# Cross attention of a decoder layer: two chunks pass each TensorE stage together, and the output projection moves in front of the second pair's scores

## Chip, cores and metric

One core of a Trainium2 chip runs the whole kernel as one program. The metric is the device time of one execution in microseconds (us), lower is better; the times shown are the median of three runs.

## The reference, cut to what matters

A decoder layer for 8 sequences of 256 tokens and width 128: a state-space block, then this cross attention, then six layers of window attention, with a layer norm after each part. Only the cross attention is touched by the change:

```python
lat = layernorm(latents, ln_l_w, ln_l_b)          # latents: x, (8, 256, 128)
ctx = layernorm(context, ln_c_w, ln_c_b)          # context: (8, 256, 128)
q = (lat @ Wq).reshape(b, n, 16, 64).transpose(0, 2, 1, 3)
k, v = jnp.split(ctx @ Wkv, 2, axis=-1)           # heads as for q
attn = jnp.clip(jnp.einsum('bhnd,bhsd->bhns', q, k) * 64 ** -0.5, -11.0, 11.0)
out = jnp.einsum('bhns,bhsd->bhnd', jax.nn.softmax(attn, axis=-1), v)
out = out.transpose(0, 2, 1, 3).reshape(b, n, 1024) @ Wo + bo
x = _layernorm(x + out, axis=-1)
```

## The kernel before

The kernel is written engine by engine: each engine has its own instruction list in an order set by hand, and semaphores alone order the engines against each other. All data is float32. TensorE (PE) writes only to PSUM; ScalarE (ACT), VectorE (DVE) and GpSimd (POOL) do the rest; SyncE (SP) issues the DMAs.

The cross attention works through 64 **chunks** g = 8b + c: batch b of 8, and chunk c of 8, which is a pair of heads (2 x 64 channels = 128 partitions). For a chunk:

- `project(g)` on PE makes q and k of the two heads (L966, L967), in one of the two "misc" PSUM banks `psM`. `copy_qk(g)` on ACT copies them to `qk[g % 2]` (L852).
- `scores(g)` on PE: keys x queries, 64 rows of the array for each head, into two of the four banks `psS` (L982). `exponentials(g)` on ACT writes `E` (L845), one of two slots; `clip(g)` on DVE limits it in place (L899), since clipping after the exponential is the same as before it.
- `sum_of_tiles(g)` on POOL adds the two tiles of keys into `Es` (L794), from which a matmul with ones makes the denominator.
- `times_v(g)` on PE: the values times E (L997), 64 columns of the array for each head, and the denominator (L1001), into one of two banks `psO`.
- `normalise(g)` on DVE: reciprocal of the denominator (L903), and the product into `OT[b % 2, c]` (L904).

For a batch: `statistics`, `deviation`, `hats` (layer norm of latents and context, on DVE and ACT), `transpose_rows` on PE (L958) and `scale_transposed` on ACT into `latT` and `ctxT`; `project_v(b, n)`, four parts, on PE (L973) with `evacuate_v` on ACT (L836); and at its end `out_projection(b, t)`, two tiles t of 128 tokens, 8 matmuls each over the 8 chunks of `OT` (L1012), `residual`, `moments2`, `deviation2`, `finish` (L909 to L918).

All that goes through a `psM` bank (transposes `cat`, `qk`, `v`, `wo`) is a *fill*. The list `fills` gives the order of them, and fill k takes bank k % 2, so each fill waits until the one two places before it was evacuated.

PE's loop over g runs one chunk ahead with projections and one behind with the values: project(g+1), scores(g), times_v(g-1). The batch work is set between: the output projection's first tile of batch b-1 after times_v at c = 1, its second before the scores at c = 2, transposes at c = 3, one value projection at each of c = 4 to 7. The first tile waits for the last normalised chunk of its batch:

```python
if t == 0:
    pe.wait_ge(O_free, (b + 1) * NC)
    ps, full = bank(b, "wo")
```

Names of tiles in the trace: `x_psM`, `x_psS`, `x_psO` are the banks, `x_latT`, `x_ctxT`, `x_qk`, `x_E`, `x_Es`, `x_V`, `x_rden`, `x_OT`, `x_res`, `x_hat` the buffers, `x_wq`, `x_wk`, `x_wv`, `x_wo` the weights. One float32 matmul of the program appears as two weight loads (PEld) and two matmul passes (PE).

Of the kernel before, what the change touches and what calls it, by code (L numbers as in the profile page):

```python
# [17 lines left out]
ALU = mybir.AluOpType  # L18
ACT = mybir.ActivationFunctionType
AX = mybir.AxisListType  # L20

P = 128
B, L, D = 8, 256, 128
TILES = B * L // P
TPB = L // P
# [3 lines left out]
H, DH = 16, 64  # L29
# [651 lines left out]
def cross_attention_block(nc, xall, ident, eps_col, inputs, window):  # L681
# [8 lines left out]
    NC = INNER // P  # L690
    R = 2 * TPB
    LOADS = 16 * 7
    CHUNKS = B * NC
    LO, HI = float(np.exp(-11.0)), float(np.exp(11.0))

    with ExitStack() as ctx:
        def sb(name, shape, dt=F32):
            return ctx.enter_context(nc.sbuf_tensor(name, shape, dt))
# [5 lines left out]
        wq, wk, wv, wo = inputs.wq, inputs.wk, inputs.wv, inputs.wo  # L704
# [8 lines left out]
        ctxT = sb("x_ctxT", [P, 2, L])  # L713
        V1 = sb("x_V1", [P, 2, TPB, H, DH])
        qk = sb("x_qk", [P, 2, 2, L])
        E = sb("x_E", [P, 2, 2, TPB, L])
        Es = sb("x_Es", [P, 2, 2, L])
        rden = sb("x_rden", [P, 2, L])
        OT = sb("x_OT", [P, 2, NC, L])
# [27 lines left out]

        block = ctx.enter_context(nc.Block())

        fills = [(0, "cat"), (0, "qk0")]  # L750
        for g in range(CHUNKS + 1):
            b, c = divmod(g, NC)
            if g + 1 < CHUNKS:
                fills.append(((g + 1) // NC, f"qk{(g + 1) % NC}"))
            if g == 0:
                fills += [(0, f"v{n}") for n in range(4)]
            if c == 1 and b >= 1:
                fills.append((b - 1, "wo"))
            if c == 3 and b + 1 < B:
                fills.append((b + 1, "cat"))  # L760
            if c >= 4 and b + 1 < B:
                fills.append((b + 1, f"v{c - 4}"))
        fills.append((B - 1, "wo"))
        place = {f: (k % 2, k // 2) for k, f in enumerate(fills)}

# [17 lines left out]
        @block.gpsimd  # L783
        def _(pool):
            pool.memset(ones[:, :], 1.0).then_inc(Es_ready, 1)
            pool.memset(window.xsA[0:1, 0, 64:D], 0.0)
            pool.wait_ge(loaded, LOADS)

            def sum_of_tiles(g):
                pool.wait_ge(E_ready, 2 * g + 2)  # L790
                if g >= 2:

                    pool.wait_ge(O_full, g - 1)
                pool.tensor_tensor(Es[:, g % 2, :, :], E[:, g % 2, :, 0, :], E[:, g % 2, :, 1, :], ALU.add).then_inc(Es_ready, 1)  # L794

            def add_bias(b):
                if b >= 1:

                    pool.wait_ge(finished, b)
                pool.tensor_tensor(res[:, :, :], xall[:, b * TPB:(b + 1) * TPB, :], bo[:, :].unsqueeze(1).broadcast_to([P, TPB, D]), ALU.add).then_inc(res_ready, 1)  # L800

            for g in range(CHUNKS):
                b, c = divmod(g, NC)
                sum_of_tiles(g)
                if c == NC - 1:
                    add_bias(b)
            pool.wait_ge(window.loaded, 32)
            pool.tensor_scalar(window.base_tab[:, :, 0, :, :], window.base_tab[:, :, 0, :, :], 8.0, None, ALU.mult)

        @block.scalar  # L810
        def _(act):
            act.preload_act_table_set(LN_EXP)
            act.wait_ge(loaded, LOADS)
            chain = Chain(act, act_chain, 0, 0)

            def deviation(b):
                act.wait_ge(mom_ready, b + 1)
                chain(act.activation(lnv[:, :], mom[:, :, 1], ACT.Ln, bias=eps_col))
                act.activation(rstd[:, :], lnv[:, :], ACT.Exp, scale=-0.5).then_inc(rstd_ready, 1)

            def deviation2(b):
                act.wait_ge(mom2_ready, b + 1)
                chain(act.activation(lnv2[:, :], mom2[:, :, 1], ACT.Ln, bias=eps_col))
                act.activation(rstd2[:, :], lnv2[:, :], ACT.Exp, scale=-0.5).then_inc(rstd2_ready, 1)

            def scale_transposed(b):
                ps, free = wait_fill(act, b, "cat")
                act.activation(ctxT[:, b % 2, :], ps[:, L:2 * L], ACT.Identity, bias=cols[:, 3:4], scale=cols[:, 2:3])
                act.activation(latT[:, b % 2, :], ps[:, 0:L], ACT.Identity, bias=cols[:, 1:2], scale=cols[:, 0:1]).then_inc(free, 1)

            def evacuate_v(b, n):
                ps, free = wait_fill(act, b, f"v{n}")
                if b >= 2 and n == 0:

                    act.wait_ge(O_full, (b - 1) * NC)
                act.activation(V1[:, b % 2, n // 2, (n % 2) * 8:(n % 2) * 8 + 8, :],  # L836
                               ps[:, :].rearrange("p (h d) -> p h d", d=DH), ACT.Copy).then_inc(free, 1)

            def exponentials(g):
                for j in range(2):  # L840
                    act.wait_ge(S_full, 2 * g + j + 1)
                    if j == 0 and g >= 2:

                        act.wait_ge(O_full, g - 1)
                    act.activation(E[:, g % 2, j, :, :], psS[(2 * g + j) % 4][:, :, :], ACT.Exp, scale=DH ** -0.5).then_inc(E_exp, 1)  # L845

            def copy_qk(g):
                ps, free = wait_fill(act, g // NC, f"qk{g % NC}")
                if g >= 2:

                    act.wait_ge(S_full, 2 * g - 2)
                act.activation(qk[:, g % 2, :, :].rearrange("p a t -> p (a t)"), ps[:, :], ACT.Copy).then_inc(free, 1)  # L852

            deviation(0)
            scale_transposed(0)
            copy_qk(0)
            for g in range(CHUNKS + 1):
                b, c = divmod(g, NC)
                if g + 1 < CHUNKS:
                    copy_qk(g + 1)  # L860
                if g < CHUNKS:
                    exponentials(g)
                if g == 0:
                    for n in range(4):
                        evacuate_v(0, n)
                if c == 1 and b + 1 < B:
                    deviation(b + 1)
                if c == 3 and b >= 1:
                    deviation2(b - 1)
                if c == 3 and b + 1 < B:  # L870
                    scale_transposed(b + 1)
                if c >= 4 and b + 1 < B:
                    evacuate_v(b + 1, c - 4)
            deviation2(B - 1)

        @block.vector
        def _(dve):
# [18 lines left out]
            def clip(g):  # L896
                for j in range(2):
                    dve.wait_ge(E_exp, 2 * g + j + 1)
                    dve.tensor_scalar(E[:, g % 2, j, :, :], E[:, g % 2, j, :, :], LO, HI, ALU.max, ALU.min).then_inc(E_ready, 1)  # L899

            def normalise(g):
                dve.wait_ge(O_full, g + 1)
# [17 lines left out]

            statistics(0)
            hats(0)
            for g in range(CHUNKS + 1):
                b, c = divmod(g, NC)
                if c == 2 and b >= 1:
                    residual(b - 1)
                if g < CHUNKS:
                    clip(g)
                if g >= 1:
                    normalise(g - 1)  # L930
                if c == 0 and b + 1 < B:
                    statistics(b + 1)
                if c == 2 and b + 1 < B:
                    hats(b + 1)
                if c == 2 and b >= 1:
                    moments2(b - 1)
                if c == 4 and b >= 1:
                    finish(b - 1)
            residual(B - 1)
            moments2(B - 1)  # L940
# [3 lines left out]
        def _(pe):  # L944
# [41 lines left out]
            def times_v(g):  # L986
# [7 lines left out]
                    pe.wait_ge(O_free, g - 1)  # L994
                for kt in range(TPB):
                    for j in range(2):
                        pe.matmul(psO[g % 2][j * DH:(j + 1) * DH, 0, :], V1[:, b % 2, kt, 2 * c + j, :], E[:, g % 2, j, kt, :],  # L997
                                  start=(kt == 0), stop=(kt == TPB - 1), skip_group_check=True)
                pe.wait_ge(Es_ready, g + 2)
                for j in range(2):  # L1000
# [14 lines left out]

            transpose_rows(0)
            project(0)
            for g in range(CHUNKS + 1):
                b, c = divmod(g, NC)
                if g + 1 < CHUNKS:  # L1020
                    project(g + 1)
                if c == 2 and b >= 1:
                    out_projection(b - 1, 1)
                if g < CHUNKS:
                    scores(g)
                if g == 0:
                    for n in range(4):
                        project_v(0, n)
                if g >= 1:
                    times_v(g - 1)  # L1030
                if c == 1 and b >= 1:
                    out_projection(b - 1, 0)
                if c == 3 and b + 1 < B:
                    transpose_rows(b + 1)
                if c >= 4 and b + 1 < B:
                    project_v(b + 1, c - 4)
            out_projection(B - 1, 0)
            out_projection(B - 1, 1)

# [973 lines left out]
```

## Time and profile before

| | |
|---|---|
| median of 3 runs | 2365.95 us (2365.91 to 2366.62) |
| profiled execution | 2364.26 us |
| its span, first to last instruction | 2362.5 us |
| PE / DVE / ACT / POOL busy | 93% / 79% / 72% / 70% |
| mean granted TensorE clock | 0.983 |
| cross attention | from about 326 us to 622 us of the span |

Shares are over the whole span, of which the cross attention is about an eighth. A matmul's end in the profile is modelled, so the start times of weight loads tell PE's pace better than durations do. PEld is the weight load, which can run ahead of the matmul before it. A bracket at the end of a line is the time the engine sat idle before it and what ended that.

### The profile page before, as it was taken

Reading aid. Unit: us, or ns where it says so; the run is one execution under the profiler, and the core shown is the slowest. Engines: PE = TensorE matmul, PEld = TensorE weight load, DVE = VectorE, ACT = ScalarE, POOL = GpSimd, SP = SyncE. Lnnn points to the kernel's source line nnn. Section 1 sums busy time; section 2 is a strip of 40 time slices with the busy share of each in tenths; the row PEclk is TensorE's granted clock in tenths of the full one; section 3 lists DMA queues with packets and bytes.
Section 4 is the critical chain, followed back from the end, with each engine's and each line's share of the span. In section 5 each row is a group of like instructions: output and inputs, shape, how many; then the busy total and the mean of one; then the engine's idle time right before and its main releaser. Section 6 shows DMA issues by size and latency. Waiting matters only on the chain. (4 is left out here: it accounts for less than half of the span.)

```text
span 2362.5 us, 70312 instructions
## 1 busy us (share of the span) xinstructions
PE 2204.0 (93%) x26385; PEld 1467.1 (62%) x26385; DVE 1860.9 (79%) x2680; ACT 1707.2 (72%) x3299; POOL 1648.2 (70%) x1553
## 2 busy tenths in 40 slices
PE   5889779999799999999999999999999999999996
PEld 3555446666456666666666666666666666666664
DVE  4899957777678878888888888888888887888884
ACT  5889734544377787787787787787778778778774
POOL 4777833333478778778788787787787787787872
PEclk8999989999999999999999999999999999999997
DMA  2311210000022222222222222222222222322221
GB/s 74 113 58 66 72 52 2 1 1 1 20 63 67 55 78 67 59 74 67 65 69 67 69 64 67 73 60 67 77 55 68 79 54 68 79 53 72 75 53 52
DMA packets 103196, 140.36 MB, mean 59 GB/s; under 512 B 63072, under 2 KB 64096, under 8 KB 102752
## 3 DMA queue, kind: packets, MB, share of 16 engines
q1 hardware_dynamic: 103136, 139.57, 21.8%
q8 instruction: 36, 0.59, 0.1%
q14 instruction: 24, 0.20, 0.0%
HBM read 56.39 MB, written 1.31 MB: 24 GB/s over the span
## 5 line engine op out<-in xcount | busy, mean ns | idle before, releaser
L1802 PE MATMUL f_psA<-f_W,f_xT 128*128 (+1 forms) x1152 | 600.7, 631 | 21.1 <-DVE f_m L1607 13.4
L1607 DVE TENSOR_TENSOR f_m<-f_psA,f_tab 128x1024 f32<-128x1024 f32 x384 | 461.1, 1222 | 119.5 <-ACT f_sq L1468 106.3
L1357 POOL TENSOR_TENSOR f_Pr<-f_Pr,f_rden 128x384 f32<-128x384 f32 x384 | 311.0, 831 | 226.2 <-DVE f_rden L1586 226.2
L1385 POOL TENSOR_TENSOR f_qkr<-f_qkr,f_rn 128x1024 f32<-128x1024 f32 x192 | 361.2, 1902 | 0.2 <-POOL f_rn L1393 0.2
L1802 PEld LDWEIGHTS f_psA<-f_W,f_xT 128*128 128x128 f32 x1152 | 188.3, 189 | 162.9 <-issue 112.5
L1468 ACT ACTIVATE f_sq<-f_psA 128x512 f32<-128x512 f32 x384 | 228.0, 594 | 78.6 <-PE f_psA L1802 75.7
L1773 PEld LDWEIGHTS f_psO<-f_PT,f_V 96*64 96x64 f32 x6144 | 203.7, 138 | 96.5 <-issue 88.4
L1375 POOL TENSOR_TENSOR f_qkr<-f_m 128x512 f32<-128x512 f32 x192 | 244.1, 1271 | 8.2 <-DVE f_m L1607 8.2
L1376 POOL TENSOR_TENSOR f_qkr<-f_m 128x512 f32<-128x512 f32 x192 | 244.5, 1273 | 0.0
L1773 PE MATMUL f_psO<-f_PT,f_V 96*64 96x64 f32 x6144 | 232.1, 228 | 1.8 <-ACT f_PT L1443 1.8
L794 POOL TENSOR_TENSOR x_Es<-x_E 128x512 f32<-128x512 f32 x64 | 81.0, 1266 | 205.8 <-DVE x_E L899 205.8
L1622 DVE TENSOR_REDUCE f_ssq<-f_sq 128x32 f32<-128x2048 f32 x96 | 218.5, 2276 | 0.0
L1460 ACT ACTIVATE f_Pr<-f_Pr 128x768 f32<-128x768 f32 x192 | 162.2, 845 | 55.4 <-DVE f_Pr L1580 53.8
L1869 PE MATMUL f_psO<-f_W,f_oT 128*128 (+1 forms) x1536 | 196.9, 281 | 0.8 <-ACT f_oT L1456 0.8
L284 POOL TENSOR_TENSOR m_Hs<-m_Hs,m_Cb 128x1024 f32<-128x1024 f32 x64 | 151.3, 2370 | 64.4 <-DVE m_Hs L472 64.4
L1452 ACT ACTIVATE f_Vt<-f_psA 128x512 f32<-128x512 f32 x192 | 114.5, 597 | 112.0 <-PE f_psA L1802 107.1
L1580 DVE TENSOR_TENSOR f_Pr<-f_psS,f_mx 128x768 f32<-128x768 f32 x192 | 183.8, 957 | 10.7
L1573 DVE TENSOR_REDUCE f_mx<-f_psS 128x8 f32<-128x768 f32 x192 | 178.3, 929 | 14.3 <-PE f_psS L1741 8.6
L1869 PEld LDWEIGHTS f_psO<-f_W,f_oT 128*128 128x128 f32 x1536 | 178.7, 191 | 7.3 <-issue 0.9
L1584 DVE TENSOR_REDUCE f_den<-f_Pr 128x8 f32<-128x768 f32 x192 | 179.9, 937 | 3.9 <-ACT f_Pr L1460 3.9
L1417 POOL TENSOR_SCALAR f_hatC<-f_xsC,f_momC,f_rstdC 128x128 f32<-128x128 f32 x96 | 77.1, 803 | 136.9 <-ACT f_rstdC L1544 136.9
L1806 PE MATMUL f_psD<-f_xnT,f_W 128*128 128x256 f32 (+1 forms) x576 | 163.6, 395 | 1.4 <-issue 0.8
(167 smaller groups left out, 4894.6 us busy)
## 6 DMA issues: line engine op xcount, KB each, us to landing
f_V<-f_Vt SPq DMA_DIRECT2D x96, 384.0 KB, 4.2
f_V<-f_Vt SPq DMA_DIRECT2D x96, 256.0 KB, 3.6
f_W<-in_f_W SPq DMA_DIRECT2D x48, 344.0 KB, 3.4
m_Cb<-m_BC_rows SPq DMA_DIRECT2D x64, 256.0 KB, 3.1
f_W<-in_f_W SPq DMA_DIRECT2D x48, 296.5 KB, 4.0
f_V<-f_Vt SPq DMA_DIRECT2D x48, 128.0 KB, 5.3
f_xsA<-xall SPq DMA_DIRECT2D x97, 32.0 KB
f_xsA<-xall SPq DMA_DIRECT2D x97, 31.8 KB
```

The lines of the kernel that those rows point to most:

```text
L1357: pool.tensor_tensor(pv, pv, rv.unsqueeze(3).broadcast_to([P, 2, 2, KEYS]), ALU.mult).then_inc(Pr_ready[g][j], 1)
L1375: pool.tensor_tensor(qv[:, :, 0, :], mv[:, 0, :, 0, :], mv[:, 1, :, 1, :], ALU.add)
L1376: pool.tensor_tensor(qv[:, :, 1, :], mv[:, 0, :, 1, :], mv[:, 1, :, 0, :], ALU.add).then_inc(rot_done[j], 1)
L1385: pool.tensor_tensor(qv, qv, rv.unsqueeze(3).broadcast_to([P, 2, GH, DH]), ALU.mult).then_inc(qkr_ready[g], 1)
L1468: act.activation(sq[:, n * 512:(n + 1) * 512], psA[n % 2][:, :], ACT.Square).then_inc(squared[n], 1)
L1580: dve.tensor_tensor(Pr[:, g, :, :].rearrange("p (a c) k -> p a c k", a=2), S4, mb, ALU.subtract).then_inc(S_free[g], 1)
L1584: dve.tensor_reduce(den[:, g, :], Pr[:, g, :, :], axis=AX.X, op=ALU.add).then_inc(den_done[g], 1)
L1607: dve.tensor_tensor(m12[:, j, :, half].rearrange("p m (h d) -> p m h d", d=DH), psA[n % 2][:, :].rearrange("p (h d) -> p h d", d=DH).unsqu ...
L1622: dve.tensor_reduce(ssq[:, :], sq[:, :].rearrange("p (h d) -> p h d", d=DH), axis=AX.X, op=ALU.add).then_inc(ssq_ready, 1)
L1773: ins = pe.matmul(psO[(h % 2) * DH:(h % 2) * DH + DH, h // 2, half * HQ:(half + 1) * HQ], V96[:, tile, half, hh_ * DH:(hh_ + 1) * DH], PT[ ...
L1802: pe.matmul(psA[n % 2][:, :], xT[:, t, :], weights(i, W_QKV + n * 512, 512), start=True, stop=True).then_inc(A_full[n_fill], 1)
L1869: ins = pe.matmul(psO[:, 0, :], oT[:, t, c, :], weights(i - 1, W_O + c * D, D), start=(c == 0), stop=(c == CH - 1))
```

## The change

All four engine lists take two chunks at a time (g, g+1; the loop step is 2). PE: scores(g), scores(g+1), times_v(g-2), times_v(g-1), project(g+2), project(g+3). `E` gets four slots, and the exponentials of chunk g wait for the values of chunk g-4 only. DVE's order in a pair is clip(g), normalise(g-2), clip(g+1), normalise(g-1). Both tiles of the output projection of batch b-1 stand in front of the scores at c = 2, directly behind the projections of the pair with c = 0. The transposes stand at c = 2, two value projections each at c = 4 and c = 6; hats and scale_transposed move to c = 2, deviation2 to c = 4, finish to c = 6. The list of fills follows.

```diff
+    ES = 4
-        E = sb("x_E", [P, 2, 2, TPB, L])
+        E = sb("x_E", [P, ES, 2, TPB, L])
...
-        fills = [(0, "cat"), (0, "qk0")]
-        for g in range(CHUNKS + 1):
+        fills = [(0, "cat"), (0, "qk0"), (0, "qk1")]
+        for g in range(0, CHUNKS + 1, 2):
             b, c = divmod(g, NC)
-            if g + 1 < CHUNKS:
-                fills.append(((g + 1) // NC, f"qk{(g + 1) % NC}"))
+            if c == 2 and b >= 1:
+                fills.append((b - 1, "wo"))
             if g == 0:
                 fills += [(0, f"v{n}") for n in range(4)]
-            if c == 1 and b >= 1:
-                fills.append((b - 1, "wo"))
-            if c == 3 and b + 1 < B:
+            if g + 2 < CHUNKS:
+                fills += [((g + 2) // NC, f"qk{(g + 2) % NC}"), ((g + 3) // NC, f"qk{(g + 3) % NC}")]
+            if c == 2 and b + 1 < B:
                 fills.append((b + 1, "cat"))
             if c >= 4 and b + 1 < B:
-                fills.append((b + 1, f"v{c - 4}"))
+                fills += [(b + 1, f"v{c - 4}"), (b + 1, f"v{c - 3}")]
...
-                    if j == 0 and g >= 2:
-                        act.wait_ge(O_full, g - 1)
+                    if j == 0 and g >= ES:
+                        act.wait_ge(O_full, g - ES + 1)
...
             deviation(0)
             scale_transposed(0)
             copy_qk(0)
-            for g in range(CHUNKS + 1):
+            copy_qk(1)
+            for g in range(0, CHUNKS + 1, 2):
                 b, c = divmod(g, NC)
-                if g + 1 < CHUNKS:
-                    copy_qk(g + 1)
                 if g < CHUNKS:
                     exponentials(g)
+                    exponentials(g + 1)
                 if g == 0:
                     for n in range(4):
                         evacuate_v(0, n)
-                if c == 1 and b + 1 < B:
+                if g + 2 < CHUNKS:
+                    copy_qk(g + 2)
+                    copy_qk(g + 3)
+                if c == 0 and b + 1 < B:
                     deviation(b + 1)
-                if c == 3 and b >= 1:
+                if c == 2 and b + 1 < B:
+                    scale_transposed(b + 1)
+                if c == 4 and b >= 1:
                     deviation2(b - 1)
-                if c == 3 and b + 1 < B:
-                    scale_transposed(b + 1)
                 if c >= 4 and b + 1 < B:
                     evacuate_v(b + 1, c - 4)
+                    evacuate_v(b + 1, c - 3)
...
             statistics(0)
             hats(0)
-            for g in range(CHUNKS + 1):
+            for g in range(0, CHUNKS + 1, 2):
                 b, c = divmod(g, NC)
+                if c == 2 and b + 1 < B:
+                    hats(b + 1)
                 if c == 2 and b >= 1:
                     residual(b - 1)
                 if g < CHUNKS:
                     clip(g)
-                if g >= 1:
+                if g >= 2:
+                    normalise(g - 2)
+                if g < CHUNKS:
+                    clip(g + 1)
+                if g >= 2:
                     normalise(g - 1)
                 if c == 0 and b + 1 < B:
                     statistics(b + 1)
-                if c == 2 and b + 1 < B:
-                    hats(b + 1)
                 if c == 2 and b >= 1:
                     moments2(b - 1)
-                if c == 4 and b >= 1:
+                if c == 6 and b >= 1:
                     finish(b - 1)
...
             transpose_rows(0)
             project(0)
-            for g in range(CHUNKS + 1):
+            project(1)
+            for g in range(0, CHUNKS + 1, 2):
                 b, c = divmod(g, NC)
-                if g + 1 < CHUNKS:
-                    project(g + 1)
                 if c == 2 and b >= 1:
+                    out_projection(b - 1, 0)
                     out_projection(b - 1, 1)
                 if g < CHUNKS:
                     scores(g)
+                    scores(g + 1)
                 if g == 0:
                     for n in range(4):
                         project_v(0, n)
-                if g >= 1:
+                if g >= 2:
+                    times_v(g - 2)
                     times_v(g - 1)
-                if c == 1 and b >= 1:
-                    out_projection(b - 1, 0)
-                if c == 3 and b + 1 < B:
+                if g + 2 < CHUNKS:
+                    project(g + 2)
+                    project(g + 3)
+                if c == 2 and b + 1 < B:
                     transpose_rows(b + 1)
                 if c >= 4 and b + 1 < B:
                     project_v(b + 1, c - 4)
+                    project_v(b + 1, c - 3)
```

In the other places where `E` is used, `g % 2` becomes `g % ES`.

## Rows read from the trace of the kernel before

**Rows 1.** The page: span, and busy us with share and instructions of each engine.

```profile
span 2362.5 us, 70312 instructions
PE 2204.0 (93%) x26385; PEld 1467.1 (62%) x26385; DVE 1860.9 (79%) x2680; ACT 1707.2 (72%) x3299; POOL 1648.2 (70%) x1553
```

**Rows 2.** Windows: length, busy PE, PEld, DVE, ACT, POOL; granted clock, DMA share, GB/s.

```profile
333.00:612.00 279.00, 278.53 (x1825) 174.45 (x1823) 207.34 (x386) 137.30 (x263) 84.57 (x71) 1.00 0.01 2
...
612.00:620.00 8.00, 5.41 (x44) 4.30 (x44) 4.17 (x4) 0.00 (x0) 2.81 (x3) 1.00 0.00 0
...
635.00:645.00 10.00, 7.45 (x34) 2.54 (x35) 5.52 (x5) 5.19 (x8) 6.52 (x5) 0.66 0.29 72
```

**Rows 3.** Waits from 333 to 612 us: us in total, times, longest.

```profile
PEld x_psO L997 <- issue: 20.9, 63, 0.3
PEld x_psM L966 <- issue: 20.7, 75, 0.4
PEld x_psS L982 <- issue: 18.3, 55, 0.4
```

**Rows 4.** Timeline of two chunks of batch 7: start us, us, engine, line, instructions.

```profile
583.91 0.30 PEld L966 LDWEIGHTS x_psM<-x_latT,x_wq 128*128 128x128 f32 x2 [0.38 <-issue]
...
584.24 0.41 PEld L967 LDWEIGHTS x_psM<-x_ctxT,x_wk 128*128 128x128 f32 x2
...
584.98 0.73 PEld L982 LDWEIGHTS x_psS<-x_qk 64*128 64x128 f32 x8 [0.33 <-issue]
...
585.08 0.60 ACT L852 ACTIVATE x_qk<-x_psM 128x512 f32<-128x512 f32 x1 [1.43 <-PE x_psM L967]
586.04 0.63 PEld L997 LDWEIGHTS x_psO<-x_E,x_V 128*64 128x64 f32 x8 [0.33 <-issue]
...
586.14 1.09 ACT L845 ACTIVATE x_E<-x_psS 128x512 f32<-128x512 f32 x2 [0.46 <-PE x_psS L982]
...
586.77 0.92 DVE L899 TENSOR_SCALAR x_E<-x_E 128x512 f32<-128x512 f32 x2 [0.52 <-ACT x_E L845]
...
587.49 1.86 PEld L1012 LDWEIGHTS x_psM<-x_wo,x_OT 128*128 128x128 f32 x16 [0.38 <-issue]
...
587.61 1.75 DVE L903 RECIPROCAL x_rden<-x_psO 128x256 f32<-128x256 f32 x1
...
589.27 0.30 PEld L966 LDWEIGHTS x_psM<-x_latT,x_wq 128*128 128x128 f32 x2
...
589.39 0.42 DVE L904 TENSOR_TENSOR x_OT<-x_psO,x_rden 128x256 f32<-128x256 f32 x1
...
592.23 0.42 DVE L909 TENSOR_TENSOR x_res<-x_res,x_psM 128x256 f32<-128x256 f32 x1 [2.41 <-PE x_psM L1012]
```

**Rows 5.** Timeline of batch 0's value projections and of batch 1's first chunks.

```profile
333.94 0.30 PEld L973 LDWEIGHTS x_psM<-x_wv,x_ctxT 128*128 128x128 f32 x2 [0.66 <-ACT x_V L836]
...
370.39 0.47 DVE L47 BATCH_NORM_STATS2 x_stats<-xall 128x6 f32<-128x128 f32 x2
...
371.40 0.38 DVE L51 BATCH_NORM_AGGREGATE x_mom<-x_stats 128x2 f32<-128x6 f32 x4
...
376.45 0.42 DVE L909 TENSOR_TENSOR x_res<-x_res,x_psM 128x256 f32<-128x256 f32 x1 [1.90 <-PE x_psM L1012]
```

**Rows 6.** Timeline of the last chunks, to the last output projection.

```profile
604.02 0.59 DVE L918 TENSOR_SCALAR xall<-x_res,x_mom,x_rstd 128x128 f32<-128x128 f32 x2
...
606.40 0.73 PEld L982 LDWEIGHTS x_psS<-x_qk 64*128 64x128 f32 x8 [0.33 <-issue]
...
611.16 0.75 DVE L899 TENSOR_SCALAR x_E<-x_E 128x512 f32<-128x512 f32 x2
611.83 1.75 DVE L903 RECIPROCAL x_rden<-x_psO 128x256 f32<-128x256 f32 x1
...
615.81 0.42 DVE L904 TENSOR_TENSOR x_OT<-x_psO,x_rden 128x256 f32<-128x256 f32 x1
616.29 3.65 PEld L1012 LDWEIGHTS x_psM<-x_wo,x_OT 128*128 128x128 f32 x32 [2.77 <-DVE x_OT L904]
```

More of the change, by code:

```diff
@@ L793, in sum_of_tiles @@
                     pool.wait_ge(O_full, g - 1)
-                pool.tensor_tensor(Es[:, g % 2, :, :], E[:, g % 2, :, 0, :], E[:, g % 2, :, 1, :], ALU.add).then_inc(Es_ready, 1)
+                pool.tensor_tensor(Es[:, g % 2, :, :], E[:, g % ES, :, 0, :], E[:, g % ES, :, 1, :], ALU.add).then_inc(Es_ready, 1)
             def add_bias(b):
@@ L841, in exponentials @@
                     act.wait_ge(S_full, 2 * g + j + 1)
-                    if j == 0 and g >= 2:
-                        act.wait_ge(O_full, g - 1)
-                    act.activation(E[:, g % 2, j, :, :], psS[(2 * g + j) % 4][:, :, :], ACT.Exp, scale=DH ** -0.5).then_inc(E_exp, 1)
+                    if j == 0 and g >= ES:
+                        act.wait_ge(O_full, g - ES + 1)
+                    act.activation(E[:, g % ES, j, :, :], psS[(2 * g + j) % 4][:, :, :], ACT.Exp, scale=DH ** -0.5).then_inc(E_exp, 1)
             def copy_qk(g):
@@ L898, in clip @@
                     dve.wait_ge(E_exp, 2 * g + j + 1)
-                    dve.tensor_scalar(E[:, g % 2, j, :, :], E[:, g % 2, j, :, :], LO, HI, ALU.max, ALU.min).then_inc(E_ready, 1)
+                    dve.tensor_scalar(E[:, g % ES, j, :, :], E[:, g % ES, j, :, :], LO, HI, ALU.max, ALU.min).then_inc(E_ready, 1)
             def normalise(g):
@@ L996, in times_v @@
                     for j in range(2):
-                        pe.matmul(psO[g % 2][j * DH:(j + 1) * DH, 0, :], V1[:, b % 2, kt, 2 * c + j, :], E[:, g % 2, j, kt, :],
+                        pe.matmul(psO[g % 2][j * DH:(j + 1) * DH, 0, :], V1[:, b % 2, kt, 2 * c + j, :], E[:, g % ES, j, kt, :],
                                   start=(kt == 0), stop=(kt == TPB - 1), skip_group_check=True)
```

## The prediction

> **What bounds the kernel now.** I read the page's busy times and granted clock first: TensorE (PE) is busy 93% of the span at a mean clock of 0.983 [rows 1]. Then the stretches of the cross attention, because the diff touches nothing else: 279 us in which PE is busy without a gap at the full clock, VectorE (DVE) 74%, ScalarE (ACT) 49%, GpSimd (POOL) 30% [rows 2]. So its price is PE's time, plus whatever pause a new order makes. Six batches, from one residual addition to the one six batches later, take 592.23 - 376.45 = 215.78 us, 35.96 each [rows 4, 5].
>
> A busy PE need not be streaming. The waits of that stretch show a pause of the weight loads, with no releaser ("issue"), in front of nearly every stage: 63 before the values, 75 before the projections, 55 before the scores [rows 3]. The timeline gives its price. First loads of one chunk: projection 583.91, scores 584.98, values 586.04, output projection 587.49, so stages of 1.06, 1.06 and 1.45 us, 3.57 in all [rows 4]. Inside a stage, 256-column passes follow each other at 0.215 us (two loads in 0.41 us, less 0.19 for one [rows 4]). Projection and scores have 4 such steps (0.86), the values with the denominator 6 (1.29). Each entry to a stage thus costs 0.20, 0.20 and 0.155 us more than staying in it: 0.555 for the three.
>
> The pause belongs to the stage, not to the chunk: the projection that follows the output projection, both 128*128, loads at 589.27 with no pause, though it is another chunk's work behind its own semaphore, while each border between 128*128, 64*128 and 128*64 has one [rows 4].
>
> The Trainium skill (TensorEngine Tiling (Array Packing), Key Properties) has a rule for this: a change of the tiling mode drains TensorE, and the trace agrees. For the size, the skill (TensorE: Matmul & The Clock Gate, Single matmul latency) puts what a lone matmul can't overlap at 166 ns at the full clock; as an estimate by that page the 93 entries below would save 15.4 us and the sum would be +5.8. The rows have the entry itself, 0.185 on average, and decide.
>
> **What the change removes.** Two chunks share each entry. Before, scores are entered 64 times, values 63; after, 32 and 31. Up to the last pair of scores, 31 entries of each kind go: 31 x 0.555 = **-17.2 us**. A pair with nothing added then takes 1.92 + 2.74 + 1.92 = 6.59 us. Number and size of matmuls, activations and vector operations are unchanged; there are no new DMAs, and SP's queue has only its wait for the first finished batch, far ahead of need.
>
> **What it adds: the wait of the output projection.** Call T the first scores load of a pair with c = 0. PE works scores(g), scores(g+1) to T+1.92, values of chunks 6 and 7 of the last batch to T+4.66, two projections to T+6.28, and now stands before the output projection, which needs the normalised chunk 7. Before, its first tile came behind a whole further chunk (PE's load of it at 587.49 shows no wait for `x_OT` [rows 4]). DVE's order is clip(g), normalise(g-2), clip(g+1), normalise(g-1):
> - The reciprocal starts 1.57 us after the values' first load (586.04 to 587.61): T+1.92+1.57 = T+3.49. clip(g), at +1.79 (584.98 to 586.77) for 0.92 us, is out of the way.
> - Reciprocal to multiplication 1.78, multiplication 0.42: T+5.69 [rows 4].
> - clip(g+1) to the next reciprocal 0.67 (611.16 to 611.83) [rows 6]: T+6.36; again 1.78 + 0.42: T+8.56; to the waiting load 0.06 (616.23 to 616.29) [rows 6]: T+8.62.
>
> The load is 8.62 - 6.28 = 2.34 us late. On-time loads stand 0.215 ahead of their matmul, the first two loads of a fresh stage only 0.11 apart (0.30 less 0.19 [rows 4]), so 0.10 is cover: a pause of 2.23 us, 7 times (the eighth is the tail): **+15.6 us**. Bounds: if the second reciprocal waited only for its matmuls (T+1.92+1.29+1.57 = 4.78, plus 2.26), the load would be due at T+7.04, pause 0.66, 4.6 us in all; if the clip pair took its 0.92 instead of 0.67, 2.5 each, 17.4. I take the chain, since program order fixes it. Nothing fills the pause: scores(g+2) is queued behind on PE, and ACT and DVE wait for those scores.
>
> **Bank waits.** The misc banks are two, and after a pair of projections the third fill (transposes at c = 2, value projection at c = 4 and 6) needs the copy of the first. That copy starts 1.17 us after the projection's first load and takes 0.60 [rows 4], and a load follows its release by 0.05 (as at 616.29, 0.06 [rows 6]): T+4.66+1.82 = 6.48 against 6.28 due. 0.2 late, 0.10 of it covered: 0.1 x 3 x 7 = **+2.1 us**, bounds 0 and 4.2. Where scores follow directly, the stage entry covers the copy (6.48 against 6.59), and the second chunk's copy ends with nothing to spare: 0.86 later, 7.34, against a load due at 6.59 + 0.76 = 7.35.
>
> **Start.** In g = 0 four value projections stand behind both pairs of exponentials (2 x 1.09 us on ACT), and they already wait for evacuations (0.66 us of load pause) [rows 5]. Evacuation starts a microsecond later, of which the second scores stage takes most: **+0.2 us**, bounds 0 and 0.6.
>
> **Tail.** From the last pair of scores, at W: normalise(60) ends W+5.69, clip(63), normalise(61) W+8.56, then finish(6), now moved here, 0.59 for its two operations [rows 6], reciprocal W+9.17, normalise(62) W+11.37, normalise(63) W+13.57, output projection W+13.63. values(62) can go at W+5.75 and values(63) at W+8.62, so they end before DVE wants them. Before, from scores(62) at 606.40 the projection came at 616.29, 9.89 later [rows 6]. At W one projection more is done (0.86) and one value stage fewer (1.29): W stands 0.43 earlier. 13.63 - 9.89 - 0.43 = **+3.3 us**; bounds 2.5 (clip and finish hidden) and 4. The tail after that is unchanged.
>
> **Edits at nothing.** Statistics (370.39 to 371.78, 1.39 us [rows 5]) run in the output projection's pause and stage: they end T+9.9, the deviation with its 0.52 us T+10.4, and hats T+11.6, before clip(g+2) is due at about T+14. Moving scale, hats, moments and finish leaves DVE its slack: its pair of clips and normalisations ends at +8.56, that is +1.97 of the next pair, where clip is due at 1.79 and the reciprocal only at 3.49; with 0.87 us of moments still 2.9. The four slots of E remove the wait of the exponentials for earlier values; ACT was not waiting for them (its wait at 586.14 is for PE's scores [rows 4]), so this only keeps the pair order possible. POOL's add_bias now waits for a later finish, about 1 us ahead of its next sum.
>
> **Sum.** -17.2 + 15.6 + 2.1 + 0.2 + 3.3 = +4.0 us. The profiled execution took 2364.26 us for its span of 2362.5 and becomes 2368.3; the median of the runs is 2365.95, 1.7 above it, and becomes **2370.0 us**.
>
> **Rivals.**
> - *The pause is covered, faster.* If normalising chunk 7 came in time, only bank waits, start and tail would stand against the saving: 2370.0 - 15.6 = 2354 us. For it: 74% DVE. Against it: two normalisations and a clip in series behind values that end at T+4.66. It decides once the pause is under 1.0 us instead of 2.23 (-11.6 + 7 x 1.0 = -4.6). Chance 0.10.
> - *The copies land late, slower.* In each pair the second chunk's scores have 0.01 us to spare, and every third fill is late already. If they came 0.2 us late in all 31 pairs: +6.2, 2376 us. For it: no slack. Against: part is hidden by the 0.10 us by which loads lead. It decides (over +4.7) from 0.03 us a pair. Chance 0.25.
> - *The clock falls in the pause, slower.* Granted clock 0.66 over 10 us right after the stage, in the window layers; but the 2.77 us wait of the load at 616.29 left it at 1.00 [rows 2, 6]. A stretch like that costs 3.4 us a batch: +24, 2394 us. Chance 0.05.
> - *The pause stays with each chunk, slower.* If nothing of it went, the price is what it adds: +21.2, 2387 us. For it: each chunk keeps its own waits. Against: the row at 589.27 [rows 4]. Chance 0.02.
> - *As forecast*, within a microsecond or two: chance 0.58. Its upper edge crosses the bound of 0.2%.
>
> **Numbers.** 0.2% (4.7 us) is about what a measurement can tell from no change. Faster: 0.10 from the first rival. Same: most of the forecast case, 0.52. Slower: the other rivals with the forecast's upper edge, 0.38. The range runs from 2362 (the low bounds of bank waits and tail, and a pause 0.8 us shorter) to 2377 (late copies on top, rival two).
>
> **What would show it.** Right: pairs without addition start scores 6.59 us apart; entries with a load pause halve; a load wait of about 2.5 us on x_OT before the output projection's first load at c = 0, seven times; PE busy no longer without gaps; the batch at about 36.2 us against 35.96; from last scores pair to last output projection 13.6 us. Wrong: an output projection that starts at once; clock below 1.00 after it; or waits of the scores on x_qk.

## The result

The change made the kernel slower: 2379.05 us median (2376.95 to 2382.38, 4 runs) against 2365.93 (2365.91 to 2366.62), ratio 1.0056, 95% interval 1.0039 to 1.0073. The forecast was 2370.0 with a range to 2377. The profiled execution took 2377.47 us, its span 2375.7 us, 13.2 more than before.

The page of the changed kernel (compare [rows 1]; each activity is nearly as before, the span is not):

```profile
span 2375.7 us, 70310 instructions
PE 2204.8 (93%) x26385; PEld 1483.7 (62%) x26385; DVE 1861.5 (78%) x2680; ACT 1704.3 (72%) x3299; POOL 1648.9 (69%) x1553
```

Its windows, columns as in [rows 2]; the first is the same stretch that had PE busy without a gap before:

```profile
333.00:612.00 279.00, 265.73 (x1758) 182.61 (x1756) 197.14 (x370) 130.54 (x255) 82.06 (x68) 0.97 0.01 2
```

PE now idles 13 us in it, and the granted clock is below 1.00, which no window of the kernel before showed there. The waits of the same stretch say at what (compare [rows 3]):

```profile
PEld x_psM L1021 <- DVE x_OT L909: 16.1, 7, 2.3
...
PE x_psM L1021 <- DVE x_OT L909: 13.3, 7, 1.9
PEld x_psM L975 <- issue: 11.2, 29, 0.4
...
PEld x_psO L1006 <- issue: 9.9, 30, 0.3
PEld x_psM L982 <- ACT x_qk L853: 9.1, 21, 0.6
```

The entries with a pause are halved (63 to 30 before the values). Seven waits of 2.3 us for `x_OT` stand before the output projection (now L1021), and 21 short ones, of the value projections, for a misc bank. (A wait of a weight load is some tenths longer than PE's own idle time, 2.3 against 1.9 here, since a load normally starts 0.2 us ahead of its matmul. Waits below are those of the loads.) The timeline of one of the seven (weight loads, and DVE's chain before it):

```profile
438.49 1.60 PEld L991 LDWEIGHTS x_psS<-x_qk 64*128 64x128 f32 x16 [0.76 <-ACT x_V L837]
...
441.98 1.76 DVE L908 RECIPROCAL x_rden<-x_psO 128x256 f32<-128x256 f32 x1 [0.78 <-PE x_psO L1010]
...
443.78 0.42 DVE L909 TENSOR_TENSOR x_OT<-x_psO,x_rden 128x256 f32<-128x256 f32 x1
...
444.12 0.75 DVE L904 TENSOR_SCALAR x_E<-x_E 128x512 f32<-128x512 f32 x2
...
444.78 1.75 DVE L908 RECIPROCAL x_rden<-x_psO 128x256 f32<-128x256 f32 x1
...
446.57 0.43 DVE L909 TENSOR_TENSOR x_OT<-x_psO,x_rden 128x256 f32<-128x256 f32 x1
...
447.05 3.65 PEld L1021 LDWEIGHTS x_psM<-x_wo,x_OT 128*128 128x128 f32 x32 [2.30 <-DVE x_OT L909]
450.82 1.17 PEld L991 LDWEIGHTS x_psS<-x_qk 64*128 64x128 f32 x12
```

From T = 438.49 the reader finds the forecast's chain: reciprocal at +3.49 (forecast 3.49), clip at +5.63 (5.69), second reciprocal +6.29 (6.36), output projection +8.56 (8.62), next scores +12.33 (by the forecast's terms 6.59 + 3.57 + 2.23 = 12.39). In five of the seven batches, though, the interval is not 12.33 but 13.95 us. Windows over the seven output projections, from their first load to the next scores:

```profile
371.13:376.53 5.40, 5.39 (x32) 5.28 (x32) 2.22 (x12) 0.50 (x2) 0.00 (x0) 0.68 0.01 2
409.09:414.49 5.40, 5.40 (x33) 5.28 (x33) 2.23 (x12) 0.50 (x2) 0.00 (x0) 0.68 0.00 0
447.05:450.82 3.77, 3.77 (x32) 3.65 (x33) 2.23 (x12) 0.50 (x2) 0.00 (x0) 1.00 0.02 4
483.38:488.78 5.40, 5.39 (x32) 5.28 (x32) 2.23 (x12) 0.50 (x2) 0.00 (x0) 0.68 0.01 3
521.34:526.74 5.40, 5.40 (x33) 5.28 (x33) 2.22 (x12) 0.50 (x2) 0.00 (x0) 0.68 0.01 5
559.30:564.70 5.40, 5.40 (x33) 5.28 (x33) 2.22 (x12) 0.50 (x2) 0.00 (x0) 0.68 0.00 0
597.26:601.02 3.76, 3.76 (x32) 3.64 (x32) 0.00 (x0) 0.00 (x0) 0.00 (x0) 1.00 0.00 0
```

The same 32 loads take 3.77 us at a granted clock of 1.00 (2.4 GHz) and 5.40 where it is 0.68 on the mean, that is, at 1.2 GHz for part of the stretch. Smaller windows over the second of the seven show when:

```profile
408.00:409.00 1.00, 0.00 (x0) 0.00 (x0) 0.96 (x3) 0.00 (x0) 0.25 (x1) 1.00 0.07 16
...
409.50:410.00 0.50, 0.50 (x5) 0.50 (x4) 0.36 (x3) 0.00 (x0) 0.00 (x0) 0.60 0.00 0
...
411.00:411.50 0.50, 0.50 (x4) 0.50 (x4) 0.50 (x3) 0.00 (x0) 0.00 (x0) 0.50 0.00 0
...
413.00:414.00 1.00, 1.00 (x11) 1.00 (x10) 0.00 (x0) 0.00 (x0) 0.00 (x0) 0.99 0.00 0
```

The clock was still at 1.00 in the pause. It fell within a microsecond of the projection's first load (409.09) and was back before the projection's end. The tail has a sixth fall (compare 616.29 in [rows 6]: 3.65 us for the same loads):

```profile
614.21 1.60 PEld L991 LDWEIGHTS x_psS<-x_qk 64*128 64x128 f32 x16 [0.33 <-ACT x_qk L853]
...
620.03 0.66 PEld L1006 LDWEIGHTS x_psO<-x_E,x_V 128*64 128x64 f32 x8 [1.54 <-issue]
...
622.83 0.66 PEld L1006 LDWEIGHTS x_psO<-x_E,x_V 128*64 128x64 f32 x8 [1.70 <-issue]
...
627.52 5.28 PEld L1021 LDWEIGHTS x_psM<-x_wo,x_OT 128*128 128x128 f32 x32 [3.61 <-DVE x_OT L909]
```

So the 13.2 us are made of six falls of the clock at 1.63 us, 9.8 in all, and 3.4 for everything else, where the forecast had 4.0 for everything. These are the falls of the one execution that was profiled; its time is 1.6 us below the median of the four.

### The profile page after: what moved, and what is told of

It reads as the page before. It is cut to its first block and busy times, and to the rows that moved or that the text cites. A ratio compares the mean times of both kernels' runs of the same rounds, so it can differ in the third digit from the quotient of the medians.

```text
span 2375.7 us, 70310 instructions
## 1 busy us (share of the span) xinstructions
PE 2204.8 (93%) x26385; PEld 1483.7 (62%) x26385; DVE 1861.5 (78%) x2680; ACT 1704.3 (72%) x3299; POOL 1648.9 (69%) x1553
## 5 line engine op out<-in xcount | busy, mean ns | idle before, releaser
L1593 DVE TENSOR_TENSOR f_Pr<-f_psS,f_mx 128x768 f32<-128x768 f32 x192 | 183.9, 958 | 10.7
L1586 DVE TENSOR_REDUCE f_mx<-f_psS 128x8 f32<-128x768 f32 x192 | 178.5, 929 | 14.4 <-PE f_psS L1754 8.6
## 6 DMA issues: line engine op xcount, KB each, us to landing
f_W<-in_f_W SPq DMA_DIRECT2D x48, 296.5 KB, 4.1
```

The lines of the kernel that those rows point to most:

```text
L1593: dve.tensor_tensor(Pr[:, g, :, :].rearrange("p (a c) k -> p a c k", a=2), S4, mb, ALU.subtract).then_inc(S_free[g], 1)
```

## The experiments

Theory A: the pause for the last normalised chunk takes back what the shared stages give, and the clock falls behind it. Rivals: the pairs cost by themselves; or the long intervals have another cause than the clock. Ratios are against runs of the kernel before on the same chip (median 2366.12 us for the first four, 2366.89 for the last three); each trace is of one execution.

**1. Output projection behind the values.**

```diff
-                if c == 2 and b >= 1:               # PE, in front of the scores
-                    out_projection(b - 1, 0)
-                    out_projection(b - 1, 1)
...
                     times_v(g - 1)
+                if c == 2 and b >= 1:
+                    out_projection(b - 1, 0)
+                    out_projection(b - 1, 1)
...
-                if c == 2 and b >= 1:               # DVE, in front of clip(g)
-                    residual(b - 1)
...
                     normalise(g - 1)
+                if c == 2 and b >= 1:
+                    residual(b - 1)
```

> The pairs stay; both tiles of the output projection go behind the values of the pair with c = 2 (before its projections), and the residual addition behind that pair's normalisations. Theory A (the loss is a 2.2 us pause in front of the output projection seven times, plus 1.63 us of half clock behind it in about five of them): both go, 2379.0 - 15.4 - 8.2 = about 2355 us, no load wait on x_OT but the last one, all pairs with c = 0 at 6.6 us. Rival B (pairing the stages costs by itself, by bank waits or by vector work that comes in bursts): the time stays above 2366 us and the pairs without additions do not come down to 6.6 us.

Measured: 2363.8 us (2362.82 to 2367.11, 11 runs), ratio 0.9994 (0.9985 to 1.0003), between the two theories. Pairs with c = 0 came down to 6.59 us and no clock fell before the tail, as A said; but the pair with c = 2 took 12.39 us instead of 10.7. Its waits show why:

```profile
PEld x_psM L974 <- DVE x_res L914: 11.5, 6, 1.9
...
PE x_psM L974 <- DVE x_res L914: 9.1, 6, 1.5
```

The second projection of the pair needs the bank of `wo`, which the residual addition frees, and I had put that behind two normalisations. That wait was of my making, and experiment 5 mends it.

**2. The pause filled with matmuls of no use.** This kernel does extra work; its output is unchanged by it.

```diff
                 if c == 2 and b >= 1:
+                    pe.wait_ge(E_exp, 2 * g - 2)
+                    for k in range(4):
+                        pe.matmul(psS[(2 * g + k % 2) % 4][:, k // 2 % 2, :], wq[:, 0:P], latT[:, b % 2, :], start=True, stop=True)
                     out_projection(b - 1, 0)
```

> The changed kernel with four 256-column matmuls of no use (wq times latT into a scores bank that is about to be overwritten) between the projections of c = 0 and the output projection: 1.7 us of work that ends before chunk 7 is normalised. The pause becomes 0.5 us of idleness, the output projection starts no earlier. Theory A: granted clock stays 1.00 in all seven, interval from scores(c = 0) to scores(c = 2) 12.3 us in all; time 2379.0 - 8.2 = about 2371 us, the drop at the last output projection stays. Rival C (the 14.0 us intervals come from something else than the clock, as contention for the OT or wo reads): time unchanged at 2379 us or up by the added work.

Measured: 2372.26 us (2366.58 to 2372.84, 11 runs), ratio 1.0021 (1.0012 to 1.0030). Timeline, weight loads of one pause:

```profile
442.03 1.70 PEld L1033 LDWEIGHTS x_psS<-x_latT,x_wq 128*128 128x128 f32 x8
444.30 3.65 PEld L1021 LDWEIGHTS x_psM<-x_wo,x_OT 128*128 128x128 f32 x32 [0.57 <-DVE x_OT L909]
448.07 1.60 PEld L991 LDWEIGHTS x_psS<-x_qk 64*128 64x128 f32 x16
```

All seven output projections took 3.77 us at clock 1.00, all seven intervals 12.32 or 12.33. Work that computes nothing made the kernel 6.8 us faster in the medians. From the first scores to the last output projection the profiled execution took 288.8 us against 296.5: five falls less, and a first pair 0.5 us longer. The output projection waits for DVE exactly as before (first load at T+8.56); only most of the idleness is gone. This shows the clock's part. In the tail, which this edit leaves alone, the clock fell as in the changed kernel, and there the 32 loads took 6.38 us.

**3. Chunk 7 normalised before the second clip.**

```diff
                 if g >= 2:
                     normalise(g - 2)
-                if g < CHUNKS:
+                if g < CHUNKS and c != 0:
                     clip(g + 1)
                 if g >= 2:
                     normalise(g - 1)
+                if g < CHUNKS and c == 0:
+                    clip(g + 1)
```

> The changed kernel; DVE at c = 0 normalises chunk 7 before the second clip. Theory A: the output projection starts 0.67 us sooner, its pause is 1.6 us instead of 2.2: 4.7 us less over seven batches, 2374 us if the clock still falls in five of seven, 2366 us if a pause of 1.6 us no longer makes it fall. If the wait of the output projection were for anything but DVE's chain (its bank, PE's own queue), no change: 2379 us.

Measured: 2364.68 us (2364.12 to 2367.39, 11 runs), ratio 0.9996 (0.9987 to 1.0005). The wait is 0.68 us shorter (1.62 against 2.30), the interval 11.65 us, and the clock stayed at 1.00 in all seven:

```profile
406.20 3.65 PEld L1023 LDWEIGHTS x_psM<-x_wo,x_OT 128*128 128x128 f32 x32 [1.62 <-DVE x_OT L909]
```

Two lines of DVE's order are worth 14.4 us in the medians. From the first scores to the last output projection the profiled execution took 12.4 us less: 4.7 for the chain and 8.1 for five falls, less 0.4 for a longer first pair. The other 2 us lie outside this stretch or between executions and aren't explained.

**4. Statistics before the second clip.**

```diff
+                if c == 0 and b + 1 < B:
+                    statistics(b + 1)
                 if g < CHUNKS:
                     clip(g + 1)
                 if g >= 2:
                     normalise(g - 1)
-                if c == 0 and b + 1 < B:
-                    statistics(b + 1)
```

> The changed kernel; DVE at c = 0 does the next batch's statistics (1.39 us) before the second clip, so chunk 7 is normalised that much later. Theory A: the pause grows to 3.6 us, seven times 1.4 = 9.8 us more; the clock falls in all seven instead of five, 3.3 us more: about 2392 us. Rival: if the drop depends on the beat of the stages and not on the pause, five of seven still fall: 2389 us.

Measured: 2378.9 us (2378.67 to 2383.7, 5 runs), ratio 1.0061 (1.0048 to 1.0075), and I was wrong. The longer chain is there (interval 13.60 us instead of 12.33), but only in six batches: the last has no statistics to do, and its wait is the old 2.29 us. The clock fell in one of the six, at a wait of the same length as in the other five, and it stayed at 1.00 behind the 2.29. One of those without a fall, then the one with:

```profile
412.53 3.65 PEld L1021 LDWEIGHTS x_psM<-x_wo,x_OT 128*128 128x128 f32 x32 [3.57 <-DVE x_OT L909]
```

```profile
373.30 5.28 PEld L1021 LDWEIGHTS x_psM<-x_wo,x_OT 128*128 128x128 f32 x32 [3.58 <-DVE x_OT L909]
```

(Both are lines of the timeline of weight loads.) So a pause is needed, by experiments 1 and 2, but its length alone does not settle whether the clock falls.

**5. As 1, the residual addition one place earlier.**

```diff
                 if g < CHUNKS:
                     clip(g + 1)
+                if c == 2 and b >= 1:
+                    residual(b - 1)
                 if g >= 2:
                     normalise(g - 1)
-                if c == 2 and b >= 1:
-                    residual(b - 1)
```

> The first experiment again, with the residual addition one place earlier on DVE: before the second normalisation instead of behind it. The trace of the first showed the second projection of c = 2 waiting 1.9 us for the bank that the residual addition frees. Theory A: that wait goes, the interval from scores(c = 2) to scores(c = 4) falls from 12.39 to 10.7 us in six batches, 2363.8 - 10 = about 2354 us. Rival B (the pairs bring bursts that cost elsewhere): the wait moves to another place and the time stays above 2360 us.

Measured: 2355.46 us (2354.42 to 2357.12, 5 runs), ratio 0.9952 (0.9939 to 0.9966). The pair with c = 2 takes 10.71 us, that with c = 0 6.59. Its timeline (PE's passes, ACT, POOL and most of DVE left out): scores directly behind the projections, the output projection without a wait for `x_OT`, the bank freed in time:

```profile
404.61 1.60 PEld L991 LDWEIGHTS x_psS<-x_qk 64*128 64x128 f32 x16 [0.33 <-ACT x_qk L853]
...
406.53 0.63 PEld L1006 LDWEIGHTS x_psO<-x_E,x_V 128*64 128x64 f32 x8 [0.33 <-issue]
...
409.27 3.65 PEld L1021 LDWEIGHTS x_psM<-x_wo,x_OT 128*128 128x128 f32 x32 [0.39 <-issue]
...
412.84 0.30 PEld L975 LDWEIGHTS x_psM<-x_latT,x_wq 128*128 128x128 f32 x2
...
413.15 0.42 DVE L914 TENSOR_TENSOR x_res<-x_res,x_psM 128x256 f32<-128x256 f32 x1
413.17 0.41 PEld L976 LDWEIGHTS x_psM<-x_ctxT,x_wk 128*128 128x128 f32 x2
...
413.63 0.38 PEld L975 LDWEIGHTS x_psM<-x_latT,x_wq 128*128 128x128 f32 x2
```

The rival that the pairs cost by themselves is out: the same pairs, with only the place of the output projection and its residual changed, are 23.6 us faster than the changed kernel and 11.4 faster than the kernel before.

**6. As 5, with a shorter tail.**

```diff
-                if g >= 2:
+                if g >= 2 and g != CHUNKS - 2:
                     normalise(g - 2)
                 if g < CHUNKS:
                     clip(g + 1)
+                if g == CHUNKS - 2:
+                    normalise(g - 2)
...
-                if c == 6 and b >= 1:
+                if c == 4 and b >= 1:
                     finish(b - 1)
```

> The same with the tail shortened: finish back at c = 4, and in the last pair both clips before the first normalisation. The forecast priced the tail at +3.3 us, most of it this chain. If that is right, from the last pair of scores to the last output projection 12.3 us instead of 13.3, and 1.0 us less than the kernel without these two edits, about 2353 us. If the tail waits for PE instead, no change.

Measured: 2353.98 us (2352.66 to 2355.79, 5 runs), ratio 0.9947 (0.9934 to 0.9961). From the last pair of scores to the last output projection 12.31 us (590.81 to 603.12) instead of 13.31; the last load's wait is 3.09 us, and the clock fell behind it as before (5.28 us for the loads); the gain over experiment 5 in the medians is 1.5 us, inside the spread of the runs, and the interval of the profile is what shows it. This is the fastest version that was run.

**7. The same pause at another beat.** This kernel too does extra work that leaves the output as it is.

```diff
                 if g + 2 < CHUNKS:
+                    if c == 6:
+                        pe.wait_ge(E_exp, 2 * g + 2)
+                        for k in range(3):
+                            pe.matmul(psS[(2 * g + 4 + k % 2) % 4][:, k // 2, :], wq[:, 0:P], latT[:, b % 2, :], start=True, stop=True)
                     project(g + 2)
                     project(g + 3)
```

> The changed kernel with three idle 256-column matmuls (1.29 us) between values and projections at c = 6: the pause stays at 2.2 us, the batch gets 1.29 us longer, about as long as in the kernel with the statistics first. If the length of the pause alone decides whether the clock falls, about five of seven fall as in the changed kernel: 2379.0 + 9.0 = 2388 us. If the place of the pause decides (the batch's beat), the number changes to almost none or all seven, as it was one of seven with statistics first: 2380 or 2391 us.

Measured: 2380.21 us (2378.48 to 2383.91, 5 runs), ratio 1.0057 (1.0043 to 1.0071). Nine microseconds of work were added and 1.2 us were seen in the median. In the profiled execution (the slowest of the five) the clock fell in two of seven:

```profile
373.83:379.22 5.39, 5.39 (x32) 5.27 (x32) 2.22 (x12) 0.50 (x2) 0.00 (x0) 0.68 0.00 2
413.08:416.85 3.77, 3.77 (x32) 3.65 (x32) 2.22 (x12) 0.50 (x2) 0.00 (x0) 1.00 0.00 0
...
601.21:606.61 5.40, 5.40 (x32) 5.28 (x33) 0.00 (x0) 0.00 (x0) 0.00 (x0) 0.68 0.01 3
```

The five left out are like the second. The wait before each is 2.29 or 2.30 us, as in the changed kernel. From the first scores to the last output projection it took 301.2 us against 296.5: 9.0 of added work, three falls less (4.9) and a first pair 0.5 longer. Without a fall a batch takes 12.33 + 7.14 + 8.46 + 9.70 = 37.6 us here, 37.6 with the statistics first, and 36.3 in the changed kernel. Equal beats had nearly equal counts (two of seven, one of six) at pauses of 2.3 and 3.6 us, and equal pauses had unequal counts (two and five) at different beats. That the beat is the cause is not shown: there is one execution of each, and no kernel was profiled often enough to tell how far the count varies by itself. What else sets it was not tried.

## Why the prediction was wrong

- **Entries to a stage, -17.2.** Right. A pair without additions takes 6.59 us against 2 x 3.57. Experiment 5 has the saving free of the pause, and its 2355.46 us stood at the forecast's rival "the pause is covered", 2354. The Trainium skill (TensorEngine Tiling (Array Packing), Key Properties) says that a change of the tiling mode drains TensorE; halving the changes is what gained here.
- **Pause before the output projection, +15.6.** Right in place, cause and size: 12.33 us against 10.16 (6.59 and the 3.57 of the output projection itself), 2.17 each, 15.2 in seven.
- **Bank waits, +2.1.** A little more. Taking twice the chunk before less 0.555, pairs with c = 2, 4 and 6 would take 6.98, 8.31 and 8.31 us (before: 3.57 + 3.96 and twice 4.43); they take 7.13, 8.46 and 8.40. That is 0.4 a batch, 2.8.
- **Tail, +3.3.** Too high by a wrong term. W was put only 0.43 us earlier, because "one projection more is done (0.86)". But both kernels have done all 64 projections before scores(62); in the kernel before, the scores at 606.40 and 608.91 are 1.06 + 1.45 = 2.51 apart, with no projection between. W stands the whole value stage, 1.29 us, earlier: 13.31 - 9.89 - 1.29 = 2.1. This error alone moved the forecast up by 0.9.
- **Start, +0.2.** From the first scores to the last output projection the kernel before takes 285.7 us, the changed one 296.5, so 10.8 more, of which five falls are 8.1. The 2.7 left against -17.2 + 15.2 + 2.8 + 2.1 = 2.9 leave -0.2. That too is the clock. It was coming up from 0.50 when the cross attention began, and the first scores fell on either side of the rise: in the kernel before at half clock (1.16 us for 8 loads against 0.73 later), in this profile of the changed kernel at full clock. That is worth 0.4, so the start itself cost about +0.2, as forecast. In the seven experiments the first 16 loads took 1.95 to 2.10 us, and their first pair 7.9 to 8.0 us instead of 7.5.

```profile
330.63 1.16 PEld L982 LDWEIGHTS x_psS<-x_qk 64*128 64x128 f32 x8 [0.65 <-issue]
```

```profile
331.06 1.60 PEld L991 LDWEIGHTS x_psS<-x_qk 64*128 64x128 f32 x16 [0.65 <-issue]
```


- **The clock, given 0.05 as a rival. This step failed.** "The 2.77 us wait of the load at 616.29 left it at 1.00" was one case, and I let it exclude seven others. The runs showed the opposite: the clock fell to half behind five of the seven pauses of 2.3 us and behind the last one of 3.6, and matmuls of no use in the pause kept it up (experiment 2). The falls are what carries the time from 2370 past the end of the range: five at 1.62 us in the stage and one of 1.63 in the tail, 9.8 us. Its price was off the other way: I took 3.4 us for each, from a stretch of another shape, where the output projection behind it loses only 1.63.
- **The other rivals.** Late copies: scores waited for `x_qk` at most a few tenths, and bare pairs stayed at 6.59, so nothing was lost there. A pause that stays with each chunk: refuted by the same 6.59.

The Trainium skill (TensorE: Matmul & The Clock Gate, Loop structure matters more than you think) says that matmuls kept back to back hold the clock and that a long wait for a DMA between them lets it drop. The trace agrees as to the cause, by experiment 2, and shows a loss also where the loads wait only 2.3 us in 36, for DVE.

## What to carry to other kernels

Sharing stages between two chunks cuts the drains, but it also moves work that waits for the slowest engine's serial chain right behind that chain: follow the chain to the load that needs its end (here T+8.6 against T+6.3), and put the consumer one stage later. Count a pause of a busy TensorE twice, once for its length and once for a clock that may fall behind it; and when a pause can't be removed, a shorter one, or matmuls of no use in it, can be worth more than their length. When a consumer is moved, look at which bank it frees and who is next in line for it (experiment 1 lost 10 us to that).

## What the runs showed of the hardware

- Between the first and the seventh output projection TensorE is otherwise unbroken. There, load waits of 2.3 us were followed by a granted clock of half in five of seven cases in the changed kernel, in two of seven in experiment 7 and not behind the one of experiment 4. At 3.6 us it was one of six (experiment 4), at 1.6 us none of seven and at 0.6 us none of seven. I had expected length to decide.
- In the tail the last output projection waits 3.60 or 3.61 us (3.09 in experiment 6), behind two shorter waits of the values (1.54 and 1.70 us in the changed kernel, 1.72 and 1.03 in experiment 6). The clock fell behind it in all eight kernels with pairs, and not in the kernel before, where the waits are 0.93, 0.72 and 2.77 us. Whether the length or the pauses close before it make this one certain was not tried.
- In the stage every fall cost the same: 32 weight loads took 5.27 or 5.28 us instead of 3.65. In the tail it was 5.22 to 5.28, and once 6.38 (experiment 2).
- The changed kernel's four runs spread over 5.4 us. The kernel before's four beside it spread over only 0.7, but its 27 beside experiments 1 to 4 over 4.2. So the spread by itself says nothing of a number of falls that differs from run to run, and only one run of each kernel was profiled.
